# Gathering the written rows by indirect DMA, and scaling keys and values at their eviction

## The reference

```
x  = bi_wkv(r=x, k=fside, v=fside, w, u, time_emb=cond)        # (4, 1024, 1024)
for _ in range(2):
    logits = rms(x, norm_pre_w) @ compete_w.T + compete_b       # (B, L, 16)
    vals, idx = top_k(swapaxes(logits, 1, 2), 4)                # per slot: 4 of 1024 rows
    wgt = softmax(vals)
    written = sum_k wgt[k] * (x @ write_w.T + write_b)[idx[k]]
    ws  = rms(ws + written, norm_post_w)                        # (B, 16, D)
    q, kk, vv = x @ wq.T + bq, ws @ wk.T + bk, ws @ wv.T + bv   # 16 heads of 64
    x_b = softmax(q kk^T / 8) vv @ out_proj_w.T + out_proj_b
    x   = rms(x + x_b, norm_post_w)
out = x_in + x
```

## Time and profile before

| what | value |
|---|---|
| median of 3 runs | 1136.23 us (1136.04 to 1138.14) |
| the profiled execution | 1136.02 us |
| its span | 1134.2 us |
| PE busy | 1052.3 us (93%) |
| DVE busy | 780.8 us (69%) |
| ACT busy | 591.9 us (52%) |
| POOL busy | 452.0 us (40%) |
| DMA, mean over the span | 173 GB/s |

### The profile page before, as it was taken

One profiled execution on the slowest core, in us unless ns is written; L12 is line 12 of the kernel. 1 busy time (PEld: TensorE's weight loads), 2 busy tenths in 40 slices (PEclk: granted clock), 3 DMA queues, 4 the chain that ended last, 5 costly groups with the idle time before them and its releaser, 6 DMA issues. The chain is left out here.

```text
span 1134.2 us, 15697 instructions
## 1 busy us (share of the span) xinstructions
PE 1052.3 (93%) x5040; PEld 591.3 (52%) x5040; DVE 780.8 (69%) x1018; ACT 591.9 (52%) x972; POOL 452.0 (40%) x204
## 2 busy tenths in 40 slices
PE   4899999999999889989999999997889899999996
PEld 1344444444444432756666666664327466666663
DVE  6999999999999632456666665664224566666664
ACT  4788878787878610335555555555102333333332
POOL 7999999999999300001111111111000033333333
PEclk9999999999999989999999999998899999999998
DMA  3343434343343166943344354331669556868664
GB/s 134 130 148 130 140 125 146 131 148 131 134 145 111 64 253 279 338 134 130 112 148 153 111 173 143 114 111 56 250 254 354 181 186 222 288 234 288 234 221 148
DMA packets 83392, 196.54 MB, mean 173 GB/s; under 512 B 6802, under 2 KB 48914, under 8 KB 80276
## 3 DMA queue, kind: packets, MB, share of 16 engines
q1 hardware_dynamic: 83348, 195.97, 49.2%
HBM read 137.22 MB, written 58.73 MB: 173 GB/s over the span
## 5 line engine op out<-in xcount | busy, mean ns | idle before, releaser
L937 PE MATMUL bank<-work 128*128 (+1 forms) x1024 | 247.7, 386 | 7.9 <-PEq L515 4.8
L961 PE MATMUL bank<-work 128*128 (+1 forms) x512 | 232.0, 596 | 2.5 <-ACT work L1061 1.8
L375 PE MATMUL bank<-work,ident 128*128 128x512 f32 x384 | 192.1, 623 | 35.1 <-DVE work L304 35.1
L937 PEld LDWEIGHTS bank<-work 128*128 128x128 f32 x1024 | 189.5, 192 | 46.8 <-issue 25.8
L1106 POOL COPY xres<-work 128x1024 f32 (+1 forms) x32 | 33.3, 1041 | 369.1 <-DVE work L1043 369.1
L1116 POOL TENSOR_TENSOR work<-work 128x1024 f32<-128x1024 f32 x32 | 75.4, 2355 | 263.2 <-DVE work L1043 263.2
L961 PEld LDWEIGHTS bank<-work 128*128 128x128 f32 x512 | 97.7, 191 | 99.1 <-issue 92.9
L375 PEld LDWEIGHTS bank<-work,ident 128*128 128x128 f32 x384 | 66.1, 191 | 141.8 <-issue 97.4
L995 DVE TENSOR_TENSOR work<-bank,sbias 128x256 f32<-128x256 f32 x64 | 27.2, 425 | 147.3 <-PE bank L937 147.3
L296 DVE SCALAR_TENSOR_TENSOR work<-work,decay 128x512 f32<-128x512 f32 x128 | 124.4, 991 | 0.2 <-PE bank L375 0.2
L375 PE MATMUL bank<-work 128*128 128x511 f32 x256 | 121.8, 599 | 0.0
(11 more groups left out here) (153 smaller groups left out, 1469.1 us busy)
## 6 DMA issues: line engine op xcount, KB each, us to landing
work<-in_kT SPq DMA_DIRECT2D x32, 512.0 KB, 3.3
work<-in_xT SPq DMA_DIRECT2D x32, 512.0 KB, 3.3
x0T_scratch<-work SPq DMA_DIRECT2D x32, 512.0 KB, 2.6
work<-x0T_scratch SPq DMA_DIRECT2D x32, 512.0 KB, 4.0
x1T_scratch<-work SPq DMA_DIRECT2D x32, 512.0 KB, 2.6
work<-x1T_scratch SPq DMA_DIRECT2D x32, 512.0 KB, 4.9
work<-in_x_nat SPq DMA_DIRECT2D x32, 512.0 KB, 4.6
out<-work SPq DMA_DIRECT2D x32, 512.0 KB, 3.0
```

Source lines behind the costliest of these rows:

```text
L375: return nc.tensor.matmul(ps[:, at:at + n], w, v, start=start, stop=not start, skip_group_check=True)
L937: last = nc.tensor.matmul(ps_s[p], xTb[p][:, c, :], Amat[:, i, :, c * 32:c * 32 + 32], start=(c == 0), stop=(c == NC - 1))
L961: last = nc.tensor.matmul(ps_o[:, cols], attT[:, k * P:(k + 1) * P], Bmat[k][:, i, cols], start=(k == 0), stop=(k == 1), skip_group_check= ...
```

## The change

**Natural copies in DRAM.** Two scratch tensors `xn_d[0]`, `xn_d[1]` hold x0 and x1 with one half row (512 numbers) in a row. In the recurrence SP stores each tile of `xres` there, in runs of 512 bytes; in tail 0 it stores each x1 tile.

**The head.** The logits live on 128 rows (32 for each batch: 16 slots, for each half of a row) in `lgT`, a tensor of its own. After the largest eight DVE looks up their places (`max_index`), and makes row numbers of `xn_d` from the first four. POOL issues four indirect DMAs, one for each k, that fetch 128 half rows each. DVE multiplies and adds them with the softmax weights to `Xb`, PE turns that (4 transposes), DVE copies it. Match, mask, row of weights and the products with x are gone. The first piece of wk is issued right behind those of write_w.

**The slot norm.** `tsum` is turned without being normed, and multiplied by norm_post_w as it is copied; ACT applies the scale of the norm when it evicts keys and values.

**Around it.** The squares get an area of their own in the recurrence, DVE multiplies logits by the scale of the norm once for each batch (`logits(b)`), and the constants get `dup`, `base`, `npostc`. In tail 0 the scaled logits of a tile go to `ldup`; PE turns them into `ps_lt` and ACT copies them to `lgT`, one tile later. Tail 0 is written out for all tiles on every engine.

```diff
@@ recurrence, SP, ACT, DVE
+                def store_natural(n):
+                    b, c = n // NC, n % NC
+                    wait(sp, nat_ev, n + 1)
+                    rows = xn_d[0].rearrange("(b u p h) c -> b h p u c", b=B, u=NC, h=2)
+                    sp.dma_start(rows[b, c // 4, :, :, c % 4 * P:c % 4 * P + P], xres[:, n, :, :])\
+                        .then_inc(xn_out[0][0], 16)
...
-                            nc.scalar.activation(lgacc[:, n // NC, :], ps_lg, ACT.Copy).then_inc(lg_ev, 1)
+                            wait(act, lg_ev, n // NC)
+                            nc.scalar.activation(rstd[:], ps_ss, ACT.Ln, bias=tiny[:, 2:3], scale=1.0 / C)\
+                                .then_inc(rln_ok, 1)
+                            wait(act, rln_ok, n // NC + 1)
+                            nc.scalar.activation(rstd[:], rstd[:], ACT.Exp, scale=-0.5).then_inc(rstd_ok, 1)
...
+                def logits(b):
+                    wait(dve, rstd_ok, b + 1)
+                    nc.vector.tensor_tensor(lgacc[:, b, :], ps_lg, rstd[:], ALU.mult).then_inc(lg_ev, 1)
...
@@ head, SP
                     piece(0, wr_T, 0)
                     piece(1, wr_T, 1)
+                    piece(2, wk_T, 0)
...
-                    for slot, w, i, free, count in ((2, wk_T, 0, wt_ps, 1), (0, wk_T, 1, wr_ps, 1),
+                    for slot, w, i, free, count in ((0, wk_T, 1, wr_ps, 1),
...
@@ head, PE
+                    keep_warm(psX, 8)
+                    pe.wait_ge(xb_ok, K)
+                    for j in range(4):
+                        last = nc.tensor.transpose(psA[:, j * P:(j + 1) * P], Xb[:, j * P:(j + 1) * P], ident[:])
                     last.then_inc(xbt_ps, 1)
...
                     keep_warm(psX, 1)
-
+                    pe.wait_ge(t2_ok, 1)
+                    unfold(psC, tsum, wst_ps)
                     pe.wait_ge(ssq_ok, 1)
...
-                    keep_warm(psX, 1)
-                    pe.wait_ge(ws_ok, 2)
-                    unfold(psC, ws, wst_ps)
...
@@ head, POOL
+                    pool.wait_ge(idx_ok, 1)
+                    for done in xn_out[t]:
+                        pool.wait_ge(done, 16 * NT // len(xn_out[t]))
+                    for k in range(K):
+                        pool.indirect_dma_start(out=rowsG[k], out_offset=None, in_=xn_d[t],
+                                                in_offset=bass.IndirectOffsetOnAxis(ap=gidx[:, k:k + 1], axis=0))\
+                            .then_inc(g_in[k], 16)
...
@@ head, ACT
-                    nc.scalar.activation(nat[0], psK, ACT.Copy).then_inc(kn_ok, 1)
+                    act.wait_ge(rs_ok, 1)
+                    nc.scalar.activation(nat[0], psK, ACT.Copy, scale=hstat[:, 2:3]).then_inc(kn_ok, 1)
...
@@ head, DVE
+                    nc.vector.max(top8[:, 0:8], lgT[:]).then_inc(dtop, 1)
                     dve.wait_ge(dtop, 1)
...
+                    nc.vector.max_index(idx8[:], top8[:, 0:8], lgT[:]).then_inc(dtop, 1)
+                    dve.wait_ge(dtop, 2)
+                    nc.vector.tensor_scalar(gidx[:], idx8[:, 0:K], 2.0, base[:, 0:1], ALU.mult, ALU.add)\
+                        .then_inc(idx_ok, 1)
...
                     dve.wait_ge(c_in, 16 * (7 if t == 0 else 2))
                     nc.vector.tensor_tensor(wbb, wbb, ws, ALU.add).then_inc(t1_ok, 1)
...
+                    dve.wait_ge(g_in[0], 16)
+                    nc.vector.tensor_scalar(Xb, rowsG[0], top8[:, 8:9], None, ALU.mult).then_inc(xb_ok, 1)
+                    for k in range(1, K):
+                        dve.wait_ge(g_in[k], 16)
+                        dve.wait_ge(xb_ok, k)
+                        nc.vector.scalar_tensor_tensor(Xb, rowsG[k], top8[:, 8 + k:9 + k], Xb, ALU.mult, ALU.add)\
+                            .then_inc(xb_ok, 1)
...
@@ tail 0, SP, PE, ACT
+                            wait(sp, x1_ok, m + 1)
+                            sp.dma_start(xn_d[1].rearrange("(m p h) c -> m p (h c)", m=NT, h=2)[m, :, :], x1s[p])\
+                                .then_inc(xn_out[1][p], 16)
...
+                        if first and exists(m - 3):
+                            b = (m - 3) // NC
+                            wait(pe, l_ok, m - 2)
+                            wait(pe, lt_ev, m - 3)
+                            nc.tensor.matmul(ps_lt[32 * b:32 * b + 32, :], ldup[1 - p][:], ident[:], start=True,
+                                             stop=True, skip_group_check=True).then_inc(lt_ps, 1)
...
+                        if first and exists(m - 3):
+                            rows, tc = slice((m - 3) // NC * 32, (m - 3) // NC * 32 + 32), (m - 3) % NC
+                            wait(act, lt_ps, m - 2)
+                            nc.scalar.activation(lgT[rows, tc * P:(tc + 1) * P], ps_lt[rows, :], ACT.Identity,
+                                                 bias=cbcol[rows, :]).then_inc(lt_ev, 1)
```

More of the change, by code:

```diff
@@ L51, in over_tiles, with build @@
         body(n, n % 2)
-def build(nc, xT, kT, x, cond, w_cols, u_cols, work_t, cw_cols, npre_cols, cb_col, wr_T, wr_b, wq, wk_T,
+def build(nc, xT, kT, x, cond, w_cols, u_cols, work_t, cw_cols, npre_cols, npost_cols, cb_col, wr_T, wr_b, wq, wk_T,
           wv_T, bq_cols, bk_cols, bv_cols, wo_T, wo_b, npost, out):
@@ L593, in _ @@
[L593 to L597 removed]
+                        for b in range(B):
+                            for q in range(Q):
+                                last = nc.tensor.matmul(psB[32 * b:32 * b + 32, q * TQ:(q + 1) * TQ],
+                                                        dup[:, q, :, :], lgacc[:, b, :], start=True, stop=True,
+                                                        skip_group_check=True)
@@ L861, in tail, with tiles @@
             ps_at, ps_l = banks[1][:, 0:256], banks[1][:, 512:640]
-            ps_l2 = banks[1][:, 640:656]
+            ps_l2, ps_lt = banks[1][:, 640:672], banks[1][:, 768:768 + P]
             ps_o, ps_x = banks[2], banks[3]
             rcp, mxp = (den16[:], mx[:]) if first else (banks[3][:, 512:528], banks[3][:, 528:544])
+            def tiles(eng, body, lag):
+                if first:
+                    for n in range(NT + lag):
+                        body(n, n % 2)
+                else:
+                    over_tiles(eng, body, lag)
             with nc.Block() as block:
@@ L968, in body @@
                             wait(pe, l_ok, m - 2)
+                            wait(pe, lt_ev, m - 2)
                             for c in range(NC):
@@ L982, in body @@
                             wait(pe, lp_ok, m - 1)
-                            nc.tensor.matmul(ps_l2, lp, fold[:], start=True, stop=True).then_inc(l2_ps, 1)
+                            nc.tensor.matmul(ps_l2, lp, fold[:].rearrange("p h s -> p (h s)"), start=True, stop=True).then_inc(l2_ps, 1)
                     scores(0, 0, 0)
                     scores(0, 0, 1)
-                    over_tiles(pe, body, 2 if first else 0)
+                    tiles(pe, body, 3 if first else 0)
                 @block.vector
@@ L1046, in _ @@
                     submax(0, 0)
-                    over_tiles(dve, body, 3 if first else 1)
+                    tiles(dve, body, 3 if first else 1)
                 @block.scalar
@@ L1094, in _ @@
                         wait_Bm(act)
-                    over_tiles(act, body, 2 if first else 1)
+                    tiles(act, body, 3 if first else 1)
                 if first:
```

191 lines of the change are left out of this document (82 added, 109 removed).

## The result

| what | before | after |
|---|---|---|
| median of the runs | 1136.13 us (1133.44 to 1138.14) | 1148.07 us (1146.57 to 1148.27) |
| span of the profiled execution | 1134.2 | 1146.3 |
| PE / DVE busy | 1052.3 / 780.8 | 1037.9 / 765.9 |

The changed kernel takes 1.0105 times as long by the medians; the measured ratio is 1.01, with a 95% interval from 1.0083 to 1.0117. It is slower by 12 us, though PE and DVE are each busy 14 to 15 us less. The forecast of 1135.5 and its range (to 1142) were both too low. Two executions on record, one of f_warm22 (1311.13 us) and one of the kernel before (1388.63 us), took far longer than all others and are left out of every number here.

A forecast was written before the change was run, and what follows sets the result against it. DVE was taken to bound the recurrence, PE both tails, and chains of waits the heads. Terms (1.0 + 1.3 + 0.9) - 1.6 + 0.2 - 2.5 = -0.7 took 1136.0, plus 0.2, to 1135.5 us; range 1128.5 to 1142.

The forecast's parts named there:

- the extra product of tail 0: First tail: one more product per tile at 0.13 us (0.11 to 0.25), x 30 = +3.9.
- The jumps: First tail: writing out the loop removes 12 jumps of 0.38 us each, -4.5.
- The end, forecast at +0.8: End of the first tail: one product and one ACT copy follow the former last work, +0.8.
- Landing of the bias: Both heads: wr_b lands 25.5 and 21.4 us after the start; the write projection starts at 30.8 and 26.7.
- the moved piece: Both heads: first wk_T piece, 2.1 MB, put ahead of the bias on SP's queue, delays its landing by 4.9.
- the price of the gathers: Both heads: 1.05 MB of gathers through already full DMA engines delay the bias by 3.0.
- The rival in which the bias overtakes the weights: Both heads: small transfers land before the 2.1 MB ahead; moved piece costs nothing, 4.9 x 2 less, 1125.7; chance 0.10.
- The rival in which the gathers are the gate: Both heads: four gathers one after another, at 6.0 each, land after the bias; each loses 5, 1145.5; chance 0.10.
- The clock: Both heads: PE idles from about 9 to 25 us after the start, then runs slower, +1.8 each (0 to 3).
- head 0's stretch at half clock: First head, key and value products: stretch after the norm's thin activity vanishes, -1.7 (0 if the clock falls all the same).
- The norm: Both heads: add to key projection falls from 5.5 to 2.4 us, -3.1; later weights take back +0.4.
- Start and loop: Recurrence: +1.0 for more constants and small DVE steps at the start, +1.3 for three DVE multiplies in the loop.

The follow-up runs named there:

- f_warm22: The changed kernel with 22 instead of 8 warm-up calls ahead of the transposes of Xb: 1148.84 us, ratio 1.0116 to the kernel before.
- g_unroll: The kernel before with its first tail written out for all tiles on every engine, nothing else: 1130.3 us, ratio 0.9958.
- d_wk_late: The changed kernel with the first piece of wk_T issued only after the four gathers have landed: 1138.67 us, ratio 1.0016 to the kernel before.

## Why the prediction was wrong

**The step that failed** is the extra product of tail 0: "the two transposes of L949, the same width, take 0.21 together ... so 0.11; with its weight load and two waits 0.13". The columns that stream were the same, but not the form. A transpose is one pass with 128 weight columns; the product is two passes with 32, between passes with 128, and both changes of width made a weight load late. It measured 0.53 in 28 tiles, 14.9 in place of 3.9 (four more of the 32 products stand in the end of the tail, below). With +11.0 on that one term the forecast would have been 1146.5. That this is within 2 us of the result is partly luck: the two heads together cost 6.9 more than forecast, and the recurrence (1.3), tail 1 (1.7) and the rest of tail 0 (2.1) as much less, but for 1.8. The upper bound of 0.25 was no bound: it came from the same row. The trace of before showed a change of width at L971 to L978, in the rows of the weight loads that I had not opened:

```profile
748.67 0.38 PEld L971 LDWEIGHTS bank<-work,cwz 128*32 128x32 f32 x16 [0.76 <-issue]
749.24 0.86 PEld L978 LDWEIGHTS bank<-ident,work 128*128 128x128 f32 x8 [0.20 <-issue]
```

**Tail 0, the rest.** The jumps were right (g_unroll). Not in the sum was the start: sixteen products at 3.69 in place of 5.38, less a longer wait for x0T, -1.35 up to the first transposes. The end, forecast at +0.8, looks as if it had held (20.0 us from the last transposes to head 1 before, 20.3 after), but by luck. The products of L961 that took 5.40 at the lower clock before, shown with g_unroll, run at full clock now:

```profile
792.89 3.70 PE L990 MATMUL bank<-work 128*128 128x512 f32 x8 [1.26 <-ACT work L1092]
```

Without that 1.7 the end costs 2.0, with four products and their copies in the chain where the prediction counted one. In sum -4.7 (loop) + 14.9 - 1.35 + 0.3 = +9.1, and nothing stays over.

**Head 0 and head 1, up to the projection.** Landing of the bias 25.4 and 20.8 (25.5 and 21.4), projection at 31.1 and 26.5 (30.8 and 26.7): right. That the moved piece is what it costs is shown by d_wk_late, and so is the price of the gathers, 2.9 for 3.0. The rival in which the bias overtakes the weights is refuted by the same landings. The rival in which the gathers are the gate was closer than its chance of 0.10 said: they land 8.6 to 13.3 us after issue and miss being the last by 1.7 and 0.5 us. It had priced them one behind the other; they are issued within 4 us and are in flight together. The estimate from the Trainium skill (DMA: Bandwidth & Descriptors, Anatomy of one DMA — SWDGE (gpsimd) path), 2.6 for each, has no term for what else the engines hold. The trace does not agree with it here: 8.6 to 13.3 beside the weights, and with 2.1 MB less beside them still 6.2 to 7.7 in head 0 and 8.6 to 9.9 in head 1.

**The clock.** Forecast +1.8 in each head, measured 2.3 and 2.7. The granted clock was 0.75 and 0.72 of full in these stretches:

```profile
837.50:847.20 9.70, 9.69 (x65) 2.35 (x65) 1.76 (x1) 0.00 (x0) 0.00 (x0) 0.72 0.26 79
428.60:438.00 9.40, 9.39 (x65) 2.33 (x65) 1.76 (x1) 0.00 (x0) 0.00 (x0) 0.75 0.26 84
```

That head 0's stretch at half clock would vanish (-1.7) was right at its place (L606, 12.20, is 7.07 and 3.64 now), but one came back at L695: 13.98, granted 0.50 at 479 to 481, where head 1 takes 12.28 for the same 28.

**The norm.** From the add to the key projection 5.5 became 2.2 us (forecast 2.4). But the weights behind it are late, and more than the 0.4 that I took: in head 0 PE waits 0.69 and 1.19 for in_wv_T, and in head 1 1.96, after which 32 products take 5.34 in place of 3.64. That is 3.7 in head 1, so the norm's gain of 3.3 is spent there. Head 0: +1.3 (start) + 2.3 (clock) - 3.3 (norm) + 0.5 (weights, less the stretch gone) + 1.7 (L695) = +2.5. Head 1: -1.8 + 2.7 - 3.3 + 3.7 = +1.3, of which 1.0 came back further on.

**Recurrence.** Start and loop were forecast at 2.3 and cost 0.3: the transposes of the last tile start at 392.89 against 392.62. The two parts of it are not alike. In the loop DVE had no room, as forecast. Three tiles, those with the multiply of a batch (L344), take 11.87 and not 11.54:

```profile
207.98 1.27 DVE L374 SCALAR_TENSOR_TENSOR work<-bank,gain,work 128x1024 f32<-128x1024 f32 x1
219.52 1.27 DVE L374 SCALAR_TENSOR_TENSOR work<-bank,gain,work 128x1024 f32<-128x1024 f32 x1
221.85 0.39 DVE L344 TENSOR_TENSOR work<-bank,rstd 128x256 f32<-128x256 f32 x1
231.38 1.27 DVE L374 SCALAR_TENSOR_TENSOR work<-bank,gain,work 128x1024 f32<-128x1024 f32 x1
```

That is 0.33 each, 1.0 for a forecast of 1.3; all other tiles stay at 11.54, so the 32 stores of natural x cost nothing, as forecast. It is the start that was wrong in sign: DVE's constants do end later (its first product starts at 12.49 instead of 10.68), but several of its operations in the first two tiles are shorter than before (the first long L316, at 24.76, took 3.40; L356, the same operation, takes 2.05 at 27.42), and the first L374 starts at 34.57 where L334 started at 35.13. Why they are shorter was not tried, so this part is luck. The end cost 1.7 instead of 0.9, its steps being as long as forecast:

```profile
395.12 0.47 ACT L301 ACTIVATE rstd<-bank,tiny 128x256 f32<-128x256 f32 x1
395.63 0.42 ACT L304 ACTIVATE rstd<-rstd 128x256 f32<-128x256 f32 x1
```

and the multiply at 396.07 (0.42). The block then ends a microsecond later in place of 0.4, and not by these steps: SP waits for the last store of x0T, issued at 392.87, which lands after 4.2 us in place of 2.6. One more natural store stands ahead of it; that this is why was not tried. In the runs with the same recurrence the stage ends between 397.5 and 398.5, so its +1.9 holds to about a microsecond.

**Tail 1**, unchanged in code, is 1.7 shorter: its first products run at full clock now.

## What to carry to other kernels

Price a product by a row of its own form: passes, weight columns, and what width stands ahead of and behind it; the weight loads' rows show the late starts. On a path that PE bounds, turn data with a transpose of full width rather than with a product against the identity. And where a change puts a gather on a critical chain, see what else the DMA engines hold at that time: issuing 2.1 MB of weights 16 to 20 us later in each head, when nobody waited for them, was worth 9 us. Last, a term that comes out near its forecast can hide two errors, as the end of tail 0 did.

## What was not expected of the hardware

- A product of 128 columns with 32 weight columns costs 0.53 us between passes of 128 weight columns, 0.20 to 0.29 beside others of its kind, and a transpose of the same data 0.11.
- A stretch at the lower clock (granted 0.50, 1.2 of 2.4 GHz) costs nearly the same at five places: 1.69 at L606 (12.20 against 10.51), 1.69 at the start of the tail (5.38 against 3.69), 1.70 at its end (5.40 against 3.70), 1.70 at L695 and 1.70 at 32 products of the value projection (5.34 against 3.64). Which of these places it falls on differs between kernels that run the same code there, and moves stages of unchanged code by 1.7 us.
- Idle time of 3.0 us ahead of the transposes and the write projection cost 1.4 us in the projection, 5.1 us cost 2.4, 10.5 us 1.7 (d_wk_late, head 1), and 15.1 and 17.4 us 2.7 and 2.3. So what it costs does not follow from the length of the gap alone.
- A gather of 128 rows of 2 KB takes POOL 0.95 us to issue (1.17 for the first of head 0) and, beside weights that fill the sixteen engines, 8.6 to 13.3 us to land.
